# Gathered expert outputs written into the normalised tokens' memory, chunk by chunk, and the gathers of the last two units tied to exponentials

## What is computed

```python
xn = _layernorm(x, axis=-1)
x = x + attn(xn) + ffn(xn)
# attn: softmax(q k^T / sqrt(32)) v, then @ Wo.T
# ffn, per token, e = expert_idx (mod(floor(xn @ wr + br), 8)):
#      relu(xn @ W1[e] + b1[e]) @ W2[e] + b2[e]
```

## Time and profile before

| | us |
|---|---|
| median of 3 runs | 505.51 (501.59 to 506.85) |
| profiled execution, device time | 505.35 |
| its span, first to last instruction | 503.5 |
| TensorE busy | 456.6 (91%) |
| DVE busy | 414.5 (82%) |
| GpSimd busy | 376.5 (75%) |
| ScalarE busy | 346.0 (69%) |
| 64 gathers, issue on GpSimd | 65.4 |

### The profile page before, as it was taken

One profiled execution on the slowest core, in us unless ns is written; L12 is line 12 of the kernel. 1 busy time (PEld: TensorE's weight loads), 2 busy tenths in 40 slices (PEclk: granted clock), 3 DMA queues, 4 the chain that ended last, 5 costly groups with the idle time before them and its releaser, 6 DMA issues.

```text
span 503.5 us, 15093 instructions
## 1 busy us (share of the span) xinstructions
PE 456.6 (91%) x4992; PEld 319.7 (63%) x4992; DVE 414.5 (82%) x883; ACT 346.0 (69%) x861; POOL 376.5 (75%) x399
## 2 busy tenths in 40 slices
PE   1868879999999999979999999998999989999967
PEld 1446445665656646658999999964665656656634
DVE  6998988778899899848888888875899898898865
ACT  3686457766777878847777777755766777687654
POOL 4755388888888888717777777757898888988952
PEclk9985899999999999989999999998999999999999
DMA  7994923565573896797878888726474566656322
GB/s 227 331 219 121 270 72 104 125 125 129 145 215 106 204 260 193 224 239 218 262 254 258 262 262 273 227 76 121 89 149 114 132 133 133 129 131 137 84 73 65
DMA packets 82826, 86.74 MB, mean 172 GB/s; under 512 B 10608, under 2 KB 66384, under 8 KB 82768
## 3 DMA queue, kind: packets, MB, share of 16 engines
q1 hardware_dynamic: 78672, 77.60, 57.2%
q0 software_dynamic: 4096, 8.40, 6.7%
HBM read 38.61 MB, written 22.04 MB: 120 GB/s over the span
## 4 chain that ended last, share of the span: by engine, by line
PE 43%; issue 16%; DVE 14%; POOL 13%; DMA 5%; ACT 4%; SPq 3%; POOLq 1%; ACTq 0%; DVEq 0%
POOL padd L592 12%; PE psum L1286 9%; PE psum L1251 8%; PE psum L1270 7%; DVE negm L990 6%; PE psum L1328 4%; PE psum L1301 4%; DMA stk<-mT 4%; SPq L326 3%; PE psum L1199 3%; PE psum L1200 2%; PE psum L1201 2%; DVE split L914 2%; ACT prob L724 2%; PE psum L1220 1%
## 5 line engine op out<-in xcount | busy, mean ns | idle before, releaser
L724 ACT ACTIVATE prob<-psum 128x512 f32<-128x512 f32 x256 | 150.2, 593 | 97.8 <-PE psum L1270 70.4
L990 DVE TENSOR_REDUCE negm<-psum 128x2 f16<-128x512 f32 x256 | 170.6, 682 | 43.3 <-PE psum L1251 36.2
L644 POOL TENSOR_TENSOR padd<-prob 128x512 f32<-128x512 f32 x104 | 126.6, 1218 | 34.6 <-ACT prob L724 26.3
L1251 PE MATMUL psum<-stk 96*128 96x256 f16 x512 | 101.6, 281 | 12.0 <-DVE negm L990 9.4
L592 POOL TENSOR_TENSOR padd<-xTl,padd 128x512 f16<-128x512 f32 x71 | 82.2, 1157 | 36.4 <-DVE padd L1100 36.4
L1270 PE MATMUL psum<-stk 97*128 97x256 f16 x512 | 97.8, 274 | 9.7 <-DMA stk<-mT 4.7
L794 ACT ACTIVATE xTl<-psum,xn_all 128x128 f32<-128x128 f32 x284 | 81.1, 369 | 27.5 <-POOL padd L592 20.7
L610 POOL DMA_INDIRECT xsort<-xn_all,pos x64 | 67.5, 1055 | 14.1 <-issue 13.5
L624 POOL DMA_INDIRECT xn_all<-ysort,pos x64 | 65.4, 1021 | 15.2 <-issue 7.7
L1251 PEld LDWEIGHTS psum<-stk 96*128 96x128 f16 x512 | 41.7, 98 | 54.6 <-DVE negm L990 25.8
L1286 PE MATMUL psum<-prob,vt 128*32 128x256 f32 x1024 | 70.5, 391 | 0.9 <-ACT prob L724 0.8
(11 more groups left out here) (166 smaller groups left out, 882.4 us busy)
## 6 DMA issues: line engine op xcount, KB each, us to landing
stk<-split SPq DMA_DIRECT2D x192, 128.0 KB
xn_all<-wsplit SPq DMA_DIRECT2D x71, 258.0 KB, 4.4
xsort<-oT SPq DMA_DIRECT2D x9, 512.0 KB, 4.9
xTh<-xsort SPq DMA_DIRECT2D x18, 256.0 KB, 4.0
ysort<-xTh SPq DMA_DIRECT2D x18, 256.0 KB, 4.2
out<-acc SPq DMA_DIRECT2D x15, 256.0 KB
acc<-x SPq DMA_DIRECT2D x3, 1024.0 KB, 8.4
xn_all<-W SPq DMA_DIRECT2D x12, 256.0 KB
```

Of the source, the lines that this page charges most:

```text
L644: nc.gpsimd.tensor_tensor(padd[:, bb, hs], prob[:, bb, hs, 0, :], prob[:, bb, hs, 1, :], ALU.add).then_inc(pool_add, 1)
L724: nc.scalar.activation(prob[:, bb, h, :, :].rearrange("p a c -> p (a c)"), bank[st_bank(u, n)], ACT.Exp, scale=SCALE).then_inc(act_exp, 1)
L990: V.tensor_reduce(negm[:, k % 2, col:col + 2], bank[n % 2].rearrange("p (a c) -> p a c", a=2), AX.X, ALU.max, negate=True).then_inc(dve_ma ...
L1251: ins = mm(bank[n % 2][:, qc * T:(qc + 1) * T], stk[0:96, s, 1, h, t0 + qc * P:t0 + (qc + 1) * P], stk[0:96, s, 0, h, t0:t0 + T], start=Tr ...
```

## The change

yg goes. Gather j (chunk j) writes to xn_all[:, j, :], a place that nothing else uses in that stage, and the two readers read there. The wait on dve_out goes. Instead, the first gather of a group with g >= 2 waits for the landing of the group g - 2, whose semaphore it shares. In units 30 and 31 each gather first waits for the exponential of its step.

```diff
-        yg = wf[:, 0:2048].bitcast(F32).rearrange("p (a c n) -> p a c n", a=2, c=4)
...
-            def gather(s, i):
-                if s >= 2 and i == 0:
-                    pool.wait_ge(dve_out, s - 1)
-                j = 4 * s + i
+            def gather(j):
+
+                g = j // 4
+                if j % 4 == 0 and g >= 2:
+                    pool.wait_ge(pool_g[g % 2], 64 * (g // 2))
                 nc.gpsimd.indirect_dma_start(
-                    out=yg[:, s % 2, i, :], out_offset=None, in_=ysort,
+                    out=xn_all[:, j, :], out_offset=None, in_=ysort,
                     in_offset=bass.IndirectOffsetOnAxis(ap=pos[:, j:j + 1], axis=0)
-                ).then_inc(pool_g[s % 2], 16)
+                ).then_inc(pool_g[g % 2], 16)
...
                     if n % 2 == 1 and u >= NU // 2:
-                        gather(u - NU // 2, n // 2)
+                        if u >= NU - 2:
+                            pool.wait_ge(act_exp, 8 * u + n + 1)
+                        gather(4 * (u - NU // 2) + n // 2)
...
                 a4 = acc[:, NC - 4:NC, :]
-                V.scalar_tensor_tensor(a4, yg[:, 1, :, :], 1.0 / (WS * WS), a4, ALU.mult, ALU.add
+                V.scalar_tensor_tensor(a4, xn_all[:, NC - 4:NC, :], 1.0 / (WS * WS), a4, ALU.mult, ALU.add
                                        ).then_inc(dve_part, 1)
...
                 a4 = acc[:, bass.ds(s * 4, 4), :]
-                V.scalar_tensor_tensor(a4, yg[:, par, :, :], 1.0 / (WS * WS), a4, ALU.mult, ALU.add
+                V.scalar_tensor_tensor(a4, xn_all[:, bass.ds(s * 4, 4), :], 1.0 / (WS * WS), a4, ALU.mult, ALU.add
                                        ).then_inc(dve_out, 1)
```

## The result

| | before | after |
|---|---|---|
| median, 22 runs each | 505.42 us | 503.78 us |
| ratio to before | | 0.9962 (0.9944 to 0.998) |
| profiled execution | 505.35 | 504.24 |
| its span | 503.5 | 502.4 |

The ratio and its interval are worked out from the executions in the faster of two states, and are not the quotient of the medians. The forecast was 506.2 us. The time moved the other way, by 0.4%, inside the range and within the 1% that had 86%.

A forecast was written before the change was run, and what follows sets the result against it. TensorE, busy 91% of the span, was the largest share of the last chain (43%). Parts 1 and 2 gave 0, part 3 +0.7: 505.35 + 0.7 = 506.05, or 506.2 us as a median; range 502.4 to 508.0.

The forecast's parts named there:

- The wait on the sum: Part 1: GpSimd's gather wait on the expert sum fired once, 4.4 us, covered by slack at L1004; removing it gives 0.
- Unit 30: the failed step: Unit 30's gathers, moved behind exponentials, land near 492 with 5 us of slack before their reader; cost 0.
- Part 3: Gathers of units 30 and 31 wait for exponentials 1, 3, 5 and 7; +0.7 us, range 0 to 1.5.
- a rival with 17%: ScalarE's 3.2 us hold before exponential 3 of unit 30 goes once gathers are spaced; 503.0 us, chance 17%.
- The tail: Unit 31's last gather waits for the last exponential, delaying L1004, the last normalisation and TensorE's last eight matmuls; +0.7 us.
- The rule on DVE's port: GpSimd cannot write descriptors while DVE holds their shared port pair; the rows allowed at most 0.3 us of hold.
- the rival at 507.4: DVE, busy in L1036, starves the last gather until 498.10, making it 1.25 us later; chance 3%.
- The collision with the maxima row: Gather packets delay unit 31's maxima row, which TensorE waits for; +3.1 us, to 509.3; chance 8%.
- The reads: Part 2: L1036 and L1004 read another address of the same size; 0, at most 0.6 us from DVE's sequencer.

The follow-up runs named there:

- e1: The changed kernel without the waits on exponentials, so the eight gathers of units 30 and 31 go back to back; 507.62 us, ratio 1.0056 to the kernel before.
- e2: The kernel before with only the waits on exponentials in units 30 and 31 added, old buffer and sum wait kept; 505.0 us, ratio 1.0006; repeated: 503.59 us, 0.9969.
- e7: The changed kernel with only unit 31's gathers each waiting for the exponential two steps earlier; 503.66 us, ratio 0.997 to the kernel before.
- e13: The changed kernel with unit 22's four gathers in a row behind its last key add (hardware loop, first pass); 505.19 us, ratio 1.0004 to the kernel before.
- e14: The changed kernel with unit 18's four gathers in a row behind its last key add (unrolled part); 509.22 us, ratio 1.0074 to the kernel before.
- e3: The changed kernel with each gather of units 30 and 31 waiting for the exponential two steps earlier; 502.79 us, ratio 0.9963 to the kernel before.
- before_again: The kernel before, unchanged, run once more for a second profile; 503.44 us, where the kernel before had 505.6 us in that set.
- after_again: The changed kernel, unaltered, measured a second time in another set; 502.73 us, ratio 0.9953 to the kernel before.
- e4: The changed kernel with waits on exponentials in unit 30 alone, unit 31's gathers in a row; 503.99 us, ratio 0.9995 to the kernel before.
- e3_again: The changed kernel with gathers of units 30 and 31 two exponentials earlier, repeated in a quick set; 499.42 us, ratio 0.9973 to the kernel before.
- e5: The changed kernel with unit 26's four gathers in a row behind its last key add (hardware loop, second pass); 503.09 us, ratio 1.0038 to the kernel before.
- e9: The changed kernel without waits on exponentials, its last eight gathers replaced by plain 64 KB transfers issued back to back; 500.1 us, ratio 0.9985 to the kernel before.
- e6: The changed kernel with a useless GpSimd addition before each of the last eight gathers instead of waits on exponentials; 508.65 us, ratio 1.0081 to the kernel before.

## Why the prediction was wrong

**The wait on the sum: size right, meaning wrong.** It had slack behind it, and its removal gains nothing (e1, e2). Inside the change "removing it gives 0" held, as the spacing came with it. By itself it would have failed: the wait cut nine gathers in two, and the homes without it and without the spacing cost 0.56% (e1).

**Unit 30: the failed step.** Part 3 costed the moved gathers by their own landing and readers only ("5 us of slack, cost 0"). It did not cost what their row does to other engines. I had seen the hold, 3.2 us on the chain without a releaser, and gave it to a rival with 17%, against it that the second burst had none beside it. That was weak: rows of four gathers went with a hold in e7, e13 and e14 and without one in the second burst of before, so one row without a hold says little. The rival's 503.0 stands against 503.78 measured, and the stated range holds the result only because it took in this rival: the sum's own was 505.5 to 507.6. The stretch fell by 3.9 and not 3.2: 2.8 us up to the start of exponential 3 (6.46 to 3.70) and 1.1 behind it (11.60 to 10.46). What a row holds back, and by what mechanism, stays open.

**The tail: the mechanism right, the size half.** I took +0.7; it measured +1.37 (6.92 to 8.29), and e3 shows that it is the late last gather. Two terms were short. The last gather was not released by the last exponential (end 494.11) but stood behind the gather of exponential 5, and started at 494.72, 0.61 us behind it and not 0.27. And it landed 2.70 us after its start, where I had read 2.2 from when the packets stop; the release of L1006 (497.42) comes later than the last packets (near 497.1). The Trainium skill, DMA: Bandwidth & Descriptors, in "Anatomy of one DMA — SWDGE (gpsimd) path", gives 2.0 us plus the bytes, an estimate of 2.15 us for 64 KB: the trace's 2.70 is above it.

**The rule on DVE's port.** The last gather's issue took 1.11 us among DVE's operations, within the 0.94 to 1.24 of before. It was no hold of DVE's length; the rival at 507.4 did not happen. The collision with the maxima row did not either. No row shows a wait for it in unit 31.

**The reads** from the homes cost nothing: DVE's busy time is 414.3 us against 414.5.

**The sum again, as the profiles have it:** hold -3.9, tail +1.4, so -2.5 us. The medians moved by 1.6, and by 2.2 in the second set. With -3.2 instead of 0 for the hold the forecast would have had the sign.

## What to carry to other kernels

Idle time with no releaser, on the chain, beside a row of indirect gathers is a term of the sum, and not a rival at 17%: price the change with it and without it. A wait that looks free may be what keeps a queue's work apart; before taking it away, ask what then runs back to back. When work is spaced by tying it to events, see that the last piece does not wait for the last event: two exponentials earlier gave the tail its 1.4 us back in the profile (e3), though the ratio stayed at 0.996. And when a change is worth 0.4%, repeat it in another set before believing the size.

## What the runs showed of the hardware

- In the sets in which the kernel before took 505 us, rows of four to nine indirect gathers of 128 rows, issued by GpSimd 0.3 to 0.5 us apart, went with idle times of ScalarE that spaced gathers did not show: 4.17 and 2.10 us before exponential 3 of unit 30 against 1.4 (before and before_again against after, after_again, e2), and at other exponentials 5.94 (e1), 2.40 (e4), 2.46 (e7) and 3.97 (e14), where the changed kernel has none, 1.12, 1.12 and 0.38. One row of four, the second of the kernel before, had none. In the sets with 500.6 us, eight in a row (e3_again) and four in a row (e5) had none.
- In such a hold TensorE issues matmuls without a wait among them up to 1.39 us apart (e1).
- TensorE's granted clock fell to 0.50 behind the longest holds, for 6.8 us in e1 and 3.4 us in e14, after it had been idle for 2.09 and 2.13 us. Behind the hold of the kernel before (2.06 us idle up to 485.63) it stayed at 1.00.
- What it is that the engines lack is not shown. TensorE's halting pace without a wait looks like missing instructions. The Trainium skill, Runtime: NRT & Kernel Launch, "Instruction fetch mechanics", says that each engine's sequencer fetches its next block of instructions by a DMA queue of its own, which is mostly hidden. In the window 375.5 to 376.0 of the burst in unit 18, inside the hold, one such packet of 16 KB starts:

```profile
q8 instruction: 1, 0.02, 18.6%
```

  But the changed kernel has one at the same place of unit 30 (482 us) with no hold. And in e1 the DMA view shows one between 480 and 482 us and none from there to 492, across the whole of the 5.94 us. The page counts 33 packets of this queue in e1 as in the kernels before and after. That speaks against a late fetch. The runs that were to tell first-run code (e5) and indirect from plain transfers (e9) fell in sets where an indirect row (e3_again) had no hold either, so they tell neither.
- A GpSimd addition of two SBUF operands beside a DVE addition of the same kind stretches the latter from 0.41 to 1.67 us (e6).
- The kernel before differs by 1% between sets (505 and 500.6 us), and a gain of 0.4% in the one kind was 0.14% (-0.14 to 0.42) in the other.
